# Adaptive-norm block with an RWKV-style scan and two local-attention layers: TensorE's scan loop written out over eight chunks, and GpSimd's fourth normalisation moved ahead of a join

## What is computed

```python
h = layernorm(x) * (1 + ca) + sa
x = x + ga * attn_ref(h)          # RWKV-7 style recurrence, 16 heads of 16
h = layernorm(x) * (1 + cb) + sb
x = x + gb * ffn_ref(h)           # two layers of local attention + gated MLP

def step(s, inp):                 # the recurrence, once per token
    q_, w_, k_, v_, a_, b_ = inp
    sa = einsum('bhij,bhj->bhi', s, a_)
    s = s * w_[:, :, None, :] + sa[..., None] * b_[:, :, None, :] + v_[..., None] * k_[:, :, None, :]
    return s, einsum('bhij,bhj->bhi', s, q_)

def _layer(x, ...):               # x2; window 128, 8 heads of 64
    q, k, v = split(shift_token(x) @ wqkv)
    q, k = rotary_xpos(l2norm(q) * qs, l2norm(k) * ksc)
    x = x + local_attention(q, k, v) @ wo       # softmax over own and previous window
    h = shift_token(x)
    h = (h - mu) / sqrt(var + 1e-05) * lg + lb
    a, g = split(h @ w1 + b1)
    return x + (a * gelu(g)) @ w2 + b2
```

## Time and profile before

| | |
|---|---|
| time, median of 3 runs | 4864.01 us (4858.03 to 4866.6) |
| the profiled execution's own time | 4857.42 us |
| its span | 4855.6 us |
| instructions in the span | 281580 |
| TensorE matmuls and weight loads | 114072 each |
| busy share PE, DVE, ACT, POOL | 90%, 69%, 61%, 47% |
| granted TensorE clock, mean | 0.959 |
| DMA | 728.62 MB, 150 GB/s |
| instruction-fetch queues | q14: 188 packets, q8: 71 packets |

### The profile page before, as it was taken

One profiled execution on the slowest core, in us unless ns is written; L12 is line 12 of the kernel. 1 busy time (PEld: TensorE's weight loads), 2 busy tenths in 40 slices (PEclk: granted clock), 3 DMA queues, 4 the chain that ended last, 5 costly groups with the idle time before them and its releaser, 6 DMA issues. The chain is left out here.

```text
span 4855.6 us, 281580 instructions
## 1 busy us (share of the span) xinstructions
PE 4353.1 (90%) x114072; PEld 3654.0 (75%) x114072; DVE 3336.5 (69%) x10277; ACT 2938.6 (61%) x8550; POOL 2292.0 (47%) x3196
## 2 busy tenths in 40 slices
PE   7888888778888888764999999999999999999998
PEld 6888888668888888653677777777777777777776
DVE  4666666568888888464666666666666777777775
ACT  4777777634444444343666666666666666666665
POOL 1222222157777777402454455544455555555553
PEclk8999999879999999887999999999999999999999
DMA  3333333467777777596667666667676666677765
GB/s 88 87 93 95 95 91 93 96 152 162 165 166 165 166 164 166 132 280 195 153 160 159 155 155 155 161 159 158 157 190 164 161 159 161 168 167 164 164 160 123
DMA packets 1454099, 728.62 MB, mean 150 GB/s; under 512 B 676624, under 2 KB 1398288, under 8 KB 1452816
## 3 DMA queue, kind: packets, MB, share of 16 engines
q1 hardware_dynamic: 1402448, 652.89, 58.1%
q10 hardware_dynamic: 51392, 73.02, 5.0%
HBM read 410.48 MB, written 315.15 MB: 149 GB/s over the span
## 5 line engine op out<-in xcount | busy, mean ns | idle before, releaser
L2354 ACT ACTIVATE l_prob<-l_prob,l_nb,l_rq 128x160 f32<-128x160 f32 x1024 | 522.3, 511 | 201.2 <-DVE l_nb L2189 200.8
L2015 POOL TENSOR_TENSOR l_k<-l_kn,l_tab 128x512 f32<-128x512 f32 x128 | 162.7, 1271 | 613.0 <-DVE l_kn L2163 613.0
L2031 POOL TENSOR_TENSOR l_prob<-l_prob,l_rinv 128x320 f32<-128x320 f32 x512 | 362.7, 719 | 53.5 <-DVE l_rinv L2171 53.3
L2560 PE MATMUL lD<-l_hid,w 128*128 128x128 f32 x3072 | 363.9, 275 | 0.0
L2560 PEld LDWEIGHTS lD<-l_hid,w 128*128 128x128 f32 x3072 | 353.3, 192 | 0.0
L2552 PEld LDWEIGHTS lA<-l_hn,w 128*128 128x128 f32 x2048 | 242.8, 195 | 110.3 <-POOL l_hn L2049 61.0
L2198 DVE STREAM_TRANSPOSE l_pb<-l_prob 128x320 f32<-128x320 f32 x512 | 250.5, 498 | 104.2 <-POOL l_prob L2031 104.2
L2025 POOL TENSOR_TENSOR l_qr<-l_q 128x512 f32<-128x512 f32 x128 | 162.5, 1269 | 329.2 <-DVE l_q L2127 329.2
L1097 POOL TENSOR_TENSOR sc_aqx<-sc_late,sc_headmask 128x256 f32<-128x256 f32 x256 | 175.4, 685 | 275.5 <-PE sc_Y L1190 274.0
L1173 PE MATMUL sc_AB<-sc_aq,sc_bkx 32*32 32x32 f32 x16384 | 256.5, 198 | 38.5 <-POOL sc_bkx L1097 28.2
L497 POOL TENSOR_TENSOR rk<-rk,bkraw 128x256 f32<-128x256 f32 x64 | 54.6, 871 | 478.0 <-DVE bkraw L383 478.0
(11 more groups left out here) (273 smaller groups left out, 13069.5 us busy)
## 6 DMA issues: line engine op xcount, KB each, us to landing
l_pT<-scratch_pz SPq DMA_DIRECT2D x1024, 128.0 KB, 3.8
scratch_pz<-l_pb SPq DMA_DIRECT2D x256, 320.0 KB, 3.0
scratch_qkz<-l_qk SPq DMA_DIRECT2D x128, 512.0 KB, 2.9
l_qkT<-scratch_qkz SPq DMA_DIRECT2D x512, 128.0 KB, 3.2
scratch_cm<-cm SPq DMA_DIRECT2D x64, 512.0 KB, 4.1
sc_early<-scratch_cm ACTq DMA_DIRECT2D x59, 512.0 KB, 4.5
scratch_tok<-vt SPq DMA_DIRECT2D x512, 48.0 KB, 1.8
scratch_part<-sc_att SPq DMA_DIRECT2D x64, 384.0 KB
```

The costliest lines, as they stand in the source:

```text
L2015: tt(k1[s][:], kn[s][:], wide(2, slice(0, DH)), ALU.mult)
L2031: tt(prob[s][:, pair], prob[s][:, pair], rinv[s][:, pair].unsqueeze(2).broadcast_to([P, 2, SPAN]), ALU.mult).then_inc(Q["pn"][s].sem, 1)
L2354: last_ = nc.scalar.activation(prob[s][:, h], prob[s][:, h], ACT.Exp, scale=rq8[s][:, h:h + 1], bias=nb[s][:, h:h + 1], accum_out=sums[s][ ...
L2560: last_ = mm(bank[s][3][:, c * P:(c + 1) * P], w2[:, m, c * P:(c + 1) * P], hid[s][:, m], start=(c == 0 and m == 0), stop=(c == CC - 1 and ...
```

## The change

TensorE's first scan loop gets a body of eight chunks (BODY = 2 * UC = 8) and so 30 passes for 120; the second loop is gone, and its 14 chunks are written out. In the local stage GpSimd normalises pair 3 before `join_dsq`, where it did so after it.

```diff
@@ -878,7 +878,7 @@
-    LEAD = 4
+    LEAD, BODY = 4, 2 * UC
@@ -1237,12 +1237,11 @@
                 value_part(0, 0)
                 pe.wait_ge(S["att_sb"].sem, S["att_sb"].after(LEAD * UC - 1))
                 pe.sem_inc(s_pass, 1)
-                with pe.Fori(0, (NU - LEAD) * UC // 2) as i:
-                    for c in range(2):
-                        chunk(2 * i + c, c, True, True)
-                with pe.Fori((NU - LEAD) * UC // 2, NU * UC // 2 - 1) as i:
-                    for c in range(2):
-                        chunk(2 * i + c, c, False, True)
+                with pe.Fori(0, (NU - LEAD) * UC // BODY) as i:
+                    for c in range(BODY):
+                        chunk(BODY * i + c, c % 2, True, True)
+                for n in range((NU - LEAD) * UC, NU * UC - 2):
+                    chunk(n, n % 2, False, True)
                 for c in range(2):
                     chunk(NU * UC - 2 + c, c, False, c == 0)
@@ -2088,10 +2087,9 @@
                         join_x1(o, um, wm_)
                     normalise(s, u, 1)
                     normalise(s, u, 2)
+                    normalise(s, u, 3)
                     if mlp:
                         join_dsq(o, um)
-                    normalise(s, u, 3)
-                    if mlp:
                         scale(o, um)
                     if fin and layer(u - 1, l):
                         add_residual(s, u - 1)
```

## The result

The changed kernel takes 6573.86 us (median of 4 runs, 6565.41 to 6599.53) for 4863.66 us before (4858.03 to 4866.6): a ratio of 1.353, with a 95% interval of 1.349 to 1.357. It is 1710 us slower; forecast were 6350 us, 1486 us slower, and a range of 5920 to 6840 us. The profiled execution is the longest of the four, with a span of 6597.7 us.

The account below looks back on a forecast made before the run. PE was taken to bound the local stage; in the scan, code fetching would bound the long body. 4857.4 us plus 1351 (loop), 53 (tail) and 84 (GpSimd's order) gave 6345, about 6350 us; range 5920 to 6840.

Parts of the forecast that it names:

- The loop's term: First scan loop: the eight-chunk body is fetched anew each pass, 21.4 stretches at 3.6 us, 77 us a pass, +1351 us.
- The tail: Scan's written-out end: about 8,200 instructions, 32 stretches at 3.7 us, 118 us for 65, +53 us.
- GpSimd's order: Local stage: join_dsq has no slack, variance comes 0.69 us later in 127 halves, little given back, +84 us.
- The rival's mechanism: Local stage: pair 3 ready 0.39 us earlier covers PE's waits for l_pT, 19 us less.
- The signs: Expected in the changed profile: 650 to 720 q8 packets, scan chunks 9 to 10 us apart, halves 20.3 us.
- Rivals 1 and 2: Scan loop: whole body stays, only the tail stops, 4972 us, 5%; or part stays, 5984 or 5734 us, 6% together.
- rival 3: Local stage: earlier pair 3 makes it faster, nothing fetched anew in the scan, 4816 us; 2% together with a 4919 us case.
- rival 4: Scan loop: each jump discards a fetch under way, or old waits add to the stops, 6570 us; 12%.

Follow-up runs that it names:

- k = 3: Kernel before, two-chunk body, first half of the products multiplied three times more in each of the first 240 chunks: 5147 us.
- k = 5: Kernel before, two-chunk body, first half of the products multiplied five times more in each of the first 240 chunks: 7813 us.
- scan alone: Changed kernel's scan (body of eight chunks, fourteen written out) with GpSimd's order as in the kernel before: 6479.8 us, ratio 1.332.
- tail alone: Kernel before with only the fourteen chunks of the scan's tail written out: 4925.2 us, ratio 1.0134.
- the kernels with the extra products: Kernel before, first half of the products multiplied three, five or eight times more: 5147, 7813 and 8588 us.
- GpSimd's order alone: Kernel before with only GpSimd's normalisation of pair 3 moved ahead of join_dsq: 4931.1 us, ratio 1.0145.
- the body of four chunks: Kernel before with only the first scan loop's body changed from two chunks to four: 6546.7 us, ratio 1.347.
- the three sizes: Kernel before, two-chunk body lengthened to 1681, 1937 and 2321 instructions by repeated products: 5147, 7813 and 8588 us.

## Why the prediction was right, and what it had wrong

**That the long body isn't held, and what that costs:** right. The change's whole direction follows from two numbers of the trace before, 160 instructions per us asked for in the scan and 256 per 3.3 to 4.3 us delivered for new code. The runs showed each step: q8 in every pass, stops on "issue" after every 254 instructions, and nearly the same body held or not on either side of a size. "Advanced Engine Details and Errata" of the Trainium skill, section "ISA Cache" (128KB on TensorE), agrees with the runs in its size: 2,048 instructions are eight blocks, and seven are held here (k = 3). That the eighth is wanted for the block ahead fits k = 5, where eight touched blocks are fetched as nine packets. The same section's "Only 2 cache lines!" doesn't fit TensorE here. The rule of "Runtime: NRT & Kernel Launch" in the Trainium skill, section "Instruction fetch mechanics" ("mostly hidden"), is refuted for the scan's pace, and holds in the local stage.

**The loop's term was undersized:** +1351 forecast, +1555 measured (scan alone less tail alone, by the medians; from the first copy of P to the 241st the traces have 2535 and 2546 us for 963, so +1571 and +1583). Its two factors were 21.4 stretches at 3.6 us; the profile has 22 at 3.86, 85.0 us for 77. The count accounts for 2 us of the 8 (the discarded packet ahead of the jump is a full one), the size for 6. I took 3.6 from the quieter rows, with the argument that the DMAs would have more room. They have (share 0.29), but the two rows at 3.99 and 4.31 were nearer. What sets the size is open in part. q8's packets in the trace of the changed kernel divide a stretch: in the median a packet goes out 1.3 us after PE's restart and takes 1.1 us, and PE starts again 1.4 us after its end. In the kernel before's first pass these are 1.1, 0.9 and 1.4 us. So the growth lies ahead of the packet and in it, not behind it. Per packet it was 3.86 at a DMA share of 0.29, 3.70 at 0.28, 3.56 at 0.20 and 0.17 in the kernels with the extra products, where a pass also has fewer waits for other engines per packet. No run separates these.

**The tail:** +53 forecast, +65 measured, 24 packets at 2.7 us for my 2.2. The term has the same fault: I took 3.7 us for each of 32 stretches, and the 12 us missing are 0.4 us a stretch.

**GpSimd's order:** +84 forecast, +71 measured. The step from 2818.77 to 2819.46 was right (20.35 less 19.65 us is 0.70), and so were the 0.45 to 0.5 us of idle time at the variance given with the run of GpSimd's order alone (65.0 us over 128 halves). The prediction's own 0.6 to 0.7 us of idle time was too long: it took all of the step for idle time. Mis-sized was what comes back: I took 3 us, from the means of two undisturbed stretches, where the wait for l_pT fell by 31. Before, that wait stands in longer halves outside those stretches too, 41.2 us over the run. The rival's mechanism existed; it was worth less than half of the price.

**The signs:** q8 has 775 packets, over the 650 to 720 named, and the chunks are 10.6 us apart, not 9 to 10. The count closes: 71, 15 for the longer first pass, 29 x 22 for the others, 24 for the tail and 27 for three halves with refetched code.

**The sum:** the two parts alone give 1620 + 71 = 1691 us, the two together 1710. The profiled execution, the longest of the four, is 1742 us longer than that of the kernel before: 1583 in the loop, 63 in the tail and 96 behind the scan, where the order alone has 73 and the three halves with refetched code are worth 22. Whether the other three executions had such halves isn't shown.

Rivals 1 and 2 (the body stays, in whole or in part) fell with the body of four chunks and the three sizes, rival 3 with the order alone; rival 4 (the fetch costs more in a loop) gave 6570 us, close to what was measured. Each jump does throw a fetch away (22 packets for 21 blocks), but not a second one, and the stretch with the jump is under two microseconds longer than the others. Whether the old waits add to the stops is part of the question left open above. That the total came this close to 6570 us is luck in part, since its added terms are not the ones measured.

## What to carry to other kernels

Before a loop's body is lengthened or written out, compare two rates: how many instructions per us the engine consumes there (counts in a busy-time row over its length) and how fast it gets through code that it runs for the first time. Where consumption is the faster, the body has to fit, with a block to spare for the one ahead; a loop that is 0.24 us slower per jump is by far the cheaper evil. And an engine's order is judged at the consumer: a 0.7 us step ahead of an operand that comes with no slack costs its full length each time, less what it gives back elsewhere (here 0.56 us a half were left of it).

## What the runs showed of the hardware that was not expected

- The edge is sharp in the scan. From seven touched blocks of 256 instructions to eight, a loop goes from 0 to 9 packets a pass and from 9.5 to 32.0 us (one execution each), and a longer body refetches all of itself, whatever its length: 3.56 to 3.86 us per packet in four kernels.
- Where a loop lies matters too: 128 semaphore increments ahead of two loops of 1655 and 1673 instructions cost 118 us, about 20 of them the increments' own, and the executions then varied by 1.3%. These loops, 20 instructions per us, were fetched anew at 17 of 24 jumps back, not at all of them.
- While PE waits for code its granted clock stands at 0.50, 1.2 GHz, so the matmuls that it does have take 236 to 238 ns for 193. Whether this costs anything in a stretch that waits for its packet anyway isn't shown: no kernel here fetched code in a whole loop at the full clock.
